# A transformer block and its expert layer on one core: the last loop slots and the router's weights in another order

## The chip, the cores and the metric

The kernel runs on 1 core of one Trainium2 chip. The metric is device time in microseconds (us); lower is better. It is told as the median of several executions, and one more execution was taken with the hardware profiler. Below, PE is TensorE, ACT is ScalarE, DVE is VectorE, POOL is GpSimd, and SP is the engine that issues most transfers.

## The reference

The input is x of 8 x 256 rows of 128 numbers. Cut to what matters:

```
h = layernorm(x) * (1 + ca) + sa
8 layers: Q, K = elu(h Wq)+1, elu(h Wk)+1;  V = Q * sum(K*v) / (Q * sum(K) + eps)
          h = layernorm(gelu(V Wo) + h) * s1 + b1
          h = layernorm(gelu(gelu(h Wf1) Wf2) + h) * s2 + b2
x = x + ga * h
h = layernorm(x) * (1 + cb) + sb
scores = softmax(h Wr) over 8 experts; the two largest of each row are its weights, the others 0
out = x + gb * (shared(h) + sum over experts e of weight[e] * (silu(h Ge) * (h Ue)) De)
```

The shared part is a gated network of the same form with 256 inner columns. It is cut in two, so that there are 10 units of one shape: units 0 and 1 are shared, units 2 to 9 are the experts. All arithmetic is in float32; some products are formed from a rounded high part and a low part of each operand.

## The kernel before

The 2048 rows are cut into 4 chunks of 512, with one chunk in work at a time on each stage. The kernel is written by hand: each engine has a program of its own, in the order in which it runs, and semaphores are the only tie between them. Nothing is reordered by a scheduler, so what stands first in an engine's program and waits also holds all that stands behind it.

**The loop.** One `slot(s, c, l, extra)` of each engine works at four stages of four chunks: `a` is s, the attention products; `b` is s-1, the attention's end; `f` is s-2, the feed-forward net; `d` is s-3, the last norm. There are 32 passes (NI), of 8 layers by 4 chunks. Slots NI and NI+1 stand behind the loop, where stages run out: slot NI has `b`, `f` and `d`, and slot NI+1 only `f` and `d`. `extra` puts work of the next part at named places of a slot.

**Names in a slot.** `ff1(j)` is one quarter of the feed-forward net's first product, in the order 2, 0, 1, 3; `ff2(j)` adds up its second product. PE transposes (`transposes`, L302, four 128 x 128 blocks) bring a norm's rows to one row per partition and back: `y` goes there, `xhB` and `xhD` are the normalised rows of the first and the last norm on their way back. A norm's statistics are `stats_of_rows` (four BN_STATS) and `variance` (five small operations on DVE), then the reciprocal root `rs` on POOL (`rstd`), then `normalize` on DVE. `keep_awake(n, ...)` is n transposes of the identity, whose result nobody reads.

**The second part.** Behind the first attention part chunk c is scaled (`scaled`, `zf`, on ACT), transposed (`zf_to_tm`), and added to the input (`residual`, on DVE). Its norm F gives `xhF`. For chunk 0, `xhF` comes from DVE; for chunks 1 to 3 from ACT (`norm_rows`, which also wants `nbias` from POOL). `norm_to_fm` transposes it, `second_norm` puts it into `hf` on ACT, and `split_h_hi` (ACT) and `split_h` (POOL) make its high and low parts. `scores` is the router's product. The softmax and the choice of two are done on DVE by `route_scores`, `route_compare`, `route_ranks` and `route_weights`, with `exponentials` on ACT. For chunk 0 these use Exp; for the others a quotient of two Silus, so that ACT keeps its table.

**The units.** The last loop goes over i = 0 to 39, with chunk c = i // 10 and unit u = i % 10. For each, PE makes `gate(i)` and `up(i)`, and `down(i - 2)`; ACT takes the Silu of the gate (`sg`); DVE multiplies (`su`), and, for an expert, once more by the weight (`sc`), which PE has spread over all partitions with `broadcast(i)` (L604). `weights_to_fm(c)` transposes the weights, and ACT's `weights(c)` copies them for `broadcast`. `down` from i = 2 on uses high and low parts: ACT copies `sc` to `sc_hi`, POOL subtracts. In the units of chunk c the router's work of chunk c+1 is done. The last chunk's last norm D is also left for the unit loop: `last_to_tm` at i = 12, `normalize("D", ...)` at 13 and `last_to_fm` at 14.

Of the kernel before, what the change touches and what calls it, by code (L numbers as in the profile page):

```python
# [13 lines left out]
P = 128  # L14
NB, L, D = 8, 256, 128
LAYERS, F = 8, 512
E = 8
# [14 lines left out]
def adaln_block(nc, x, w_qkv, w_o, w_f1, w_f2, v_a, v_bo, v_ln1, v_bf1, v_bf2, v_ln2, c_t, w_mod,  # L32
                w_router, w_unit, ident_in, select_in, lower_in, out):

    with ExitStack() as ctx:
# [261 lines left out]
        def _(pe):  # L297
# [38 lines left out]
            def slot(s, c, l, extra=None):  # L336
# [103 lines left out]
                if has(f):  # L440
                    ff1(2)
                    ff1(0)
                if has(b):
# [23 lines left out]
                if has(f):  # L467
                    ff2(1)
                    ff2(2)
                    ff2(3)  # L470
                if has(d) and not has(b):
                    last_norm_to_fm()
                run(extra, "behind ff2")
# [151 lines left out]
            keep_awake(10, ps_v)  # L625
            norm_to_fm(0)
            pe.wait_ge(x_new, 1)
            keep_awake(9, ps_q)
            slot(NI + 1, 1, LAYERS, {"start": scores_0, "behind ff2": unit_0})


            for i in range(CH * U):
# [6 lines left out]
                if i:  # L639
                    gate(i)  # L640
                    up(i)
                    if u == 1:
                        weights_to_fm(c)
                    if i == U + 4:
                        last_to_fm()
# [30 lines left out]
        def _(act):  # L676
# [111 lines left out]
            def norm_rows(c):  # L788
                q = buf("F", c)
                act.wait_ge(nbias_ready, c)  # L790
                act.wait_ge(to_fm["F"], c)
# [23 lines left out]
            def exponentials(c):  # L815
                act.wait_ge(lg_ready, 2 * c + 1)
                if c == 0:
                    nc.scalar.activation(ex[:], lg[:], ACT.Exp).then_inc(ex_ready, 1)
                else:

                    nc.scalar.activation(ex[:], lg[:], ACT.Silu, bias=ones[:, 1:2])
                    nc.scalar.activation(exn[:], lg[:], ACT.Silu, bias=ones[:, 0:1], scale=-1.0).then_inc(ex_ready, 1)
# [18 lines left out]
            def first_scores():  # L841
                second_norm(0)
                split_h_hi(0)
                exponentials(0)
# [5 lines left out]
            slot(NI + 1, 1, LAYERS, {"start": first_scores, "before the last norm": lambda: split_weights_hi(ORDER[7:])})  # L850
            act.wait_ge(ff2_mm, NI)
            nc.scalar.activation(g2[:], ps_f0[:], ACT.Gelu_apprx_tanh, bias=vbf2[:, 0:1]).then_inc(g2_ready, 1)
            for i in range(CH * U):
# [16 lines left out]
                if i == U + 4:  # L870
# [8 lines left out]
                if u == 1:  # L879
                    weights(c)  # L880
                if u == 1 and c:
                    mixture_sum(c - 1)
                if i == 1:
                    scaled(1)
# [14 lines left out]
        def _(pool):  # L899
# [55 lines left out]
            slots(pool, slot, None, {"start": lambda: rstd("I", CH - 1)}, {"start": lambda: split_x_lo(CH - 1, 0)})  # L955
# [7 lines left out]

            def split_h(c):
# [10 lines left out]
            slot(NI, 0, LAYERS, {"end": lambda: rstd("F", 0)})  # L975
# [27 lines left out]
        def _(dve):  # L1003
# [7 lines left out]
            def variance(k, n, eps):  # L1011
# [15 lines left out]
                if k == "F" and n:  # L1027
# [167 lines left out]
            STEPS = 7  # L1195

            def first_step(c):
                return STEPS * c + 2 * max(c - 1, 0)
# [13 lines left out]
            def second_norm(c):  # L1212
                normalize("F", c, x0[:, c])
# [11 lines left out]
            def route_scores(c):  # L1225
                n = first_step(c)
# [7 lines left out]
            def route_compare(c):  # L1234
                n = first_step(c)
# [6 lines left out]
            def route_ranks(c):  # L1242
                n = first_step(c)
# [3 lines left out]
                if c:  # L1247
                    step(n + 4, nc.vector.reciprocal(exn[:], exn[:]))
                    step(n + 5, nc.vector.tensor_tensor(ex[:], ex[:], exn[:], ALU.mult))
                step(n + 4 + 2 * bool(c), nc.vector.tensor_reduce(sm[:], ex[:], AX_X, ALU.add))  # L1250
                nc.vector.reciprocal(rsm[:], sm[:])
                step(n + 5 + 2 * bool(c), nc.vector.scalar_tensor_tensor(out=comb[:], in0=rank[:], scalar=1.5, in1=ex[:],
                                                           op0=ALU.is_lt, op1=ALU.mult))

            def route_weights(c):
                n = first_step(c)
                step(n + 6 + 2 * bool(c), nc.vector.tensor_tensor(comb2[:], comb[:], rsm[:].unsqueeze(2).to_broadcast([P, T, E]),
# [4 lines left out]
                step(n + 7 + 2 * bool(c), nc.vector.tensor_copy(cs[:, :, 0, :].bitcast(F32R), comb2[:]))  # L1262
# [129 lines left out]
```

## Time and profile before

| | |
|---|---|
| median of 3 executions | 525.33 us (525.21 to 526.71) |
| profiled execution | 526.34 us, of which the span is 524.1 us |
| PE busy | 504.4 us, 96% of the span |
| DVE busy | 429.8 us, 82% |
| ACT busy | 405.2 us, 77% |
| POOL busy | 294.6 us, 56% |

The span goes from the first to the last instruction in the trace; 2.24 us lie around it. The loop's slots take about 12 us each. Slot NI begins on PE near 388 us, slot NI+1 near 401 us, the units near 410 us. A matmul's duration in the rows includes the time until its result has landed, and several are under way at once, so the pace is read from start to start.

### The profile page before, as it was taken

The numbers are of one execution on the slowest core, as the hardware profiler recorded it, in microseconds if no ns is written. First come the engines' busy times: TensorE is split into PE (matmuls) and PEld (weight loads), VectorE is DVE, ScalarE is ACT, GpSimd is POOL, SyncE is SP. The second block draws the span as 40 slices with busy tenths as digits, with TensorE's granted clock in tenths as the row PEclk, the third lists the DMA queues.
The fourth block names the chain that finished last, engine by engine and source line by source line (L and its number), as shares of the span: only waits on it lengthen the run. The fifth ranks groups of instructions, "written<-read, shape, count | busy, mean of one in ns | idle before, by whom it ended". The sixth has DMA issues, their size and how long they took to land.

```text
span 524.1 us, 8271 instructions
## 1 busy us (share of the span) xinstructions
PE 504.4 (96%) x1996; PEld 309.3 (59%) x1996; DVE 429.8 (82%) x1633; ACT 405.2 (77%) x603; POOL 294.6 (56%) x327
## 2 busy tenths in 40 slices
PE   7789999999999999999999999999989899899997
PEld 5345565555555555655555555556546477677785
DVE  5889888988898888889888988888887667777754
ACT  4758888888888888888888888888889666657452
POOL 4435655566565666555665656655556376555552
PEclk9989999999999999999999999999999999999999
DMA  8200010001000000100010000001000000000000
GB/s 249 88 16 1 7 41 15 0 5 40 15 5 20 20 15 5 40 15 0 5 40 15 5 20 20 15 5 40 1 0 1 2 0 1 21 1 21 2 21 20
DMA packets 16070, 11.22 MB, mean 21 GB/s; under 512 B 8220, under 2 KB 13852, under 8 KB 16052
## 3 DMA queue, kind: packets, MB, share of 16 engines
q1 hardware_dynamic: 15188, 10.29, 7.1%
q10 hardware_dynamic: 864, 0.73, 0.4%
q8 instruction: 7, 0.11, 0.1%
q14 instruction: 11, 0.09, 0.1%
HBM read 9.96 MB, written 1.05 MB: 21 GB/s over the span
## 4 chain that ended last, share of the span: by engine, by line
PE 82%; DVE 8%; issue 3%; POOL 3%; ACT 2%; DMA 1%; DVEq 0%; POOLq 0%; ACTq 0%
PE bank L436 20%; PE bank L427 15%; PE bank L302 12%; PE bank L448 6%; PE bank L424 5%; PE bank L344 4%; PE bank L349 4%; PE bank L345 4%; PE bank L544 2%; PE bank L546 2%; PE bank L545 2%; PE bank L604 1%; DVE sc L1327 1%; PE bank L589 1%; PE bank L590 1%
## 5 line engine op out<-in xcount | busy, mean ns | idle before, releaser
L436 PE MATMUL bank<-hid,wf 128*128 128x512 f32 x256 | 120.2, 592 | 0.0
L913 POOL TENSOR_TENSOR rsD<-veD,c_half 128x4 f32<-128x4 f32 x32 | 37.3, 1166 | 102.1 <-DVE veD L1025 102.1
L427 PE MATMUL bank<-x,wf 128*128 128x512 f32 x192 | 93.6, 597 | 0.0
L751 ACT ACTIVATE hid<-bank,vbf 128x512 f32<-128x512 f32 x128 | 77.6, 694 | 0.2 <-PE bank L427 0.2
L436 PEld LDWEIGHTS bank<-hid,wf 128*128 128x128 f32 x256 | 46.1, 190 | 46.5 <-issue 31.1
L996 POOL TENSOR_TENSOR xs_lo<-sc,xs_hi 128x512 fp32r<-128x512 f32 x36 | 46.7, 1296 | 45.3 <-ACT xs_hi L869 44.0
L427 PEld LDWEIGHTS bank<-x,wf 128*128 128x128 f32 x192 | 35.3, 191 | 33.4 <-issue 16.3
L1115 DVE TENSOR_SCALAR x<-bank,vln 128x256 f32<-128x256 f32 x64 | 31.9, 540 | 23.8 <-PE bank L302 23.8
L1044 DVE TENSOR_SCALAR xhB<-bank,meanB,rsB 128x128 f32<-128x128 f32 x128 | 43.7, 404 | 8.8 <-POOL rsB L913 8.8
L721 ACT ACTIVATE g<-bank,vbf 128x512 f32<-128x512 f32 x31 | 21.4, 691 | 35.6 <-PE bank L436 35.6
L1044 DVE TENSOR_SCALAR xhD<-bank,meanD,rsD 128x128 f32<-128x128 f32 x128 | 43.7, 404 | 5.0 <-POOL rsD L913 0.7
L302 PEld LDWEIGHTS bank<-ident,y 128*128 128x128 f32 x256 | 29.5, 140 | 26.9 <-POOL y L933 12.9
L344 PE MATMUL bank<-xs_hi,wqkv_hi 128*128 128x512 f32 x87 | 43.7, 502 | 0.9
L933 POOL TENSOR_TENSOR y<-g,xs 128x512 f32<-128x512 f32 x32 | 40.9, 1277 | 6.4 <-ACT g L745 6.3
L913 POOL TENSOR_TENSOR rsB<-veB,c_half 128x4 f32<-128x4 f32 x32 | 32.9, 1028 | 19.7 <-DVE veB L1025 19.7
L745 ACT ACT_TABLE_LOAD x32 | 41.1, 1283 | 0.6
L928 POOL TENSOR_TENSOR y<-g,x 128x512 f32<-128x512 f32 x31 | 39.8, 1283 | 1.8 <-ACT g L721 1.8
L302 PE MATMUL bank<-ident,y 128*128 128x128 f32 x256 | 39.8, 278 | 0.8 <-POOL y L933 0.8
L724 ACT ACT_TABLE_LOAD x31 | 39.8, 1283 | 0.5
L921 POOL TENSOR_TENSOR xs_lo<-xs,xs_hi 128x512 fp32r<-128x512 f32 x29 | 38.3, 1322 | 2.5 <-ACT xs_hi L703 2.5
L448 PE MATMUL bank<-vt,wo 128*128 128x512 f32 x64 | 34.9, 627 | 0.6 <-DVE vt L1131 0.6
L424 PE MATMUL bank<-x,wf 128*128 128x256 f32 x128 | 34.0, 389 | 0.7 <-DVE x L1115 0.7
(178 smaller groups left out, 1181.2 us busy)
## 6 DMA issues: line engine op xcount, KB each, us to landing
wf<-in_w_f SPq DMA_DIRECT2D x16, 256.0 KB, 2.6
wu<-in_w_unit SPq DMA_DIRECT2D x10, 192.0 KB
wqkv<-in_w_qkv SPq DMA_DIRECT2D x7, 192.0 KB, 2.3
x<-in_x SPq DMA_DIRECT2D x4, 256.0 KB, 5.2
out<-ot SPq DMA_DIRECT2D x3, 256.0 KB, 2.2
wo<-in_w_o SPq DMA_DIRECT2D x8, 64.0 KB, 1.8
wmod<-in_w_mod ACTq DMA_DIRECT2D x1, 256.0 KB, 5.4
vln<-in_v_ln SPq DMA_DIRECT2D x16, 1.0 KB, 1.7
```

The source lines that it names most:

```text
L302: mm = nc.tensor.transpose(out_bank[:, j * P:(j + 1) * P], t, ident[:])
L344: nc.tensor.matmul(bank[:], wqkv_hi[:, w], xs_hi[c][:], start=True, stop=False)
L424: mm = nc.tensor.matmul(half(ps_ff[2], h), wf1[:, 2 * P:3 * P], half(x2[(c - 2) % CH], h), start=True, stop=True)
L427: mm = nc.tensor.matmul(ps_ff[j][:], wf1[:, j * P:(j + 1) * P], x2[(c - 2) % CH][:], start=True, stop=True)
L436: mm = nc.tensor.matmul(ps_f0[:], wf2[:, j, :], hid[:, j, :], start=(j == 0), stop=(j == FJ - 1))
L448: nc.tensor.matmul(ps_b[:], wo[:], vt[(c - 1) % CH][:], start=True, stop=True).then_inc(wo_mm, 1)
L745: nc.scalar.activation(g1[:], ps_b[:], ACT.Gelu_apprx_tanh, bias=vbo[:, 0:1]).then_inc(g1_ready, 1)
L751: nc.scalar.activation(hid[:, j, :], ps_ff[j][:], ACT.Gelu_apprx_tanh, bias=vbf1[:, j:j + 1]).then_inc(h_ready, 1)
L913: nc.gpsimd.tensor_tensor(rs[buf(k, n)][:], ve[buf(k, n)][:], c_half[:], ALU.pow).then_inc(rstd_ready[k], 1)
L933: nc.gpsimd.tensor_tensor(y1[:], g1[:], xs[(c - 1) % CH][:], ALU.add).then_inc(y1_ready, 1)
L996: nc.gpsimd.tensor_tensor(sc_lo[k % 2][:], sc[i % 3][:], sc_hi[k % 2][:].bitcast(F32), ALU.subtract).then_inc(sc_lo_ready, 1)
L1044: ap = nc.vector.tensor_scalar(rows_of(k, n)[:, j, :], src[:, j, :], mean[q][:, j:j + 1], rs[q][:, j:j + 1], ALU.subtract, ALU.mult)
```

## The change

**First norm ahead.** In slot NI, DVE's `residual(0)` now stands ahead of the last norm's `normalize`, and the variance of chunk 0's norm F behind that of norm B. POOL does `rs` of B, then `rs` of F and `nbias`. On PE, ten and nine identity transposes become twelve ahead of `xhB` and four behind it; `norm_to_fm(0)` moves from ahead of slot NI+1 into its `ff1`, and the router's product from the slot's start to behind `ff2`.

**Rows by ACT, Silus.** Chunk 0's `xhF` now comes from ACT at the start of slot NI+1; `second_norm(0)` and `split_h_hi(0)` stand behind the first of its four gelus. The Exp, with its table, goes; two Silus stand behind the last gelu. `scaled(1)` moves ahead of that gelu. `weights_to_fm(0)` moves from unit 1 to unit 2.

**Three groups.** `route_ranks` loses its second half to the new `route_sums`, which stands behind the products of the eighth unit, and `route_weights` moves behind those of the ninth. DVE's last `normalize("D", ...)` moves from i = 13 to 14, and PE's `last_to_fm` and ACT's eviction from 14 to 15.

```diff
--- before.py
+++ after.py
@@ -442,0 +443 @@
+                run(extra, "within ff1")
@@ -470,0 +472 @@
+                run(extra, "behind ff2")
@@ -473 +475 @@
-                run(extra, "behind ff2")
+                run(extra, "behind the last norm")
@@ -625,5 +627,7 @@
-            keep_awake(10, ps_v)
-            norm_to_fm(0)
-            pe.wait_ge(x_new, 1)
-            keep_awake(9, ps_q)
-            slot(NI + 1, 1, LAYERS, {"start": scores_0, "behind ff2": unit_0})
+            keep_awake(12, ps_v)
+
+            def awake_0():
+                keep_awake(4, ps_v)
+
+            slot(NI + 1, 1, LAYERS, {"start": awake_0, "within ff1": lambda: norm_to_fm(0),
+                                     "behind ff2": scores_0, "behind the last norm": unit_0})
@@ -642 +646 @@
-                    if u == 1:
+                    if i == 2 or (c and u == 1):
@@ -644 +648 @@
-                    if i == U + 4:
+                    if i == U + 5:
@@ -790,2 +794,3 @@
-                act.wait_ge(nbias_ready, c)
-                act.wait_ge(to_fm["F"], c)
+                act.wait_ge(nbias_ready, c + 1)
+                if c:
+                    act.wait_ge(to_fm["F"], c)
@@ -817,6 +822,2 @@
-                if c == 0:
-                    nc.scalar.activation(ex[:], lg[:], ACT.Exp).then_inc(ex_ready, 1)
-                else:
-
-                    nc.scalar.activation(ex[:], lg[:], ACT.Silu, bias=ones[:, 1:2])
-                    nc.scalar.activation(exn[:], lg[:], ACT.Silu, bias=ones[:, 0:1], scale=-1.0).then_inc(ex_ready, 1)
+                nc.scalar.activation(ex[:], lg[:], ACT.Silu, bias=ones[:, 1:2])
+                nc.scalar.activation(exn[:], lg[:], ACT.Silu, bias=ones[:, 0:1], scale=-1.0).then_inc(ex_ready, 1)
@@ -841 +842 @@
-            def first_scores():
+            def first_rows():
@@ -844 +845,4 @@
-                exponentials(0)
+
+            def last_splits():
+                split_weights_hi(ORDER[7:])
+                scaled(1)
@@ -850 +854,2 @@
-            slot(NI + 1, 1, LAYERS, {"start": first_scores, "before the last norm": lambda: split_weights_hi(ORDER[7:])})
+            slot(NI + 1, 1, LAYERS, {"start": lambda: norm_rows(0), "after the first gelu": first_rows,
+                                     "before the last norm": last_splits})
@@ -852,0 +858 @@
+            exponentials(0)
@@ -870 +876 @@
-                if i == U + 4:
+                if i == U + 5:
@@ -879 +885 @@
-                if u == 1:
+                if i == 2 or (c and u == 1):
@@ -883,2 +888,0 @@
-                if i == 1:
-                    scaled(1)
@@ -955 +958,0 @@
-            slots(pool, slot, None, {"start": lambda: rstd("I", CH - 1)}, {"start": lambda: split_x_lo(CH - 1, 0)})
@@ -963,0 +967 @@
+            slots(pool, slot, None, {"start": lambda: rstd("I", CH - 1)}, {"start": lambda: split_x_lo(CH - 1, 0)})
@@ -975 +979,3 @@
-            slot(NI, 0, LAYERS, {"end": lambda: rstd("F", 0)})
+            slot(NI, 0, LAYERS)
+            rstd("F", 0)
+            norm_bias(0)
@@ -1027 +1033 @@
-                if k == "F" and n:
+                if k == "F":
@@ -1195,4 +1201 @@
-            STEPS = 7
-
-            def first_step(c):
-                return STEPS * c + 2 * max(c - 1, 0)
+            STEPS = 9
@@ -1212,2 +1214,0 @@
-            def second_norm(c):
-                normalize("F", c, x0[:, c])
@@ -1226 +1227 @@
-                n = first_step(c)
+                n = STEPS * c
@@ -1235 +1236 @@
-                n = first_step(c)
+                n = STEPS * c
@@ -1243 +1244 @@
-                n = first_step(c)
+                n = STEPS * c
@@ -1247,4 +1248,6 @@
-                if c:
-                    step(n + 4, nc.vector.reciprocal(exn[:], exn[:]))
-                    step(n + 5, nc.vector.tensor_tensor(ex[:], ex[:], exn[:], ALU.mult))
-                step(n + 4 + 2 * bool(c), nc.vector.tensor_reduce(sm[:], ex[:], AX_X, ALU.add))
+                step(n + 4, nc.vector.reciprocal(exn[:], exn[:]))
+                step(n + 5, nc.vector.tensor_tensor(ex[:], ex[:], exn[:], ALU.mult))
+
+            def route_sums(c):
+                n = STEPS * c
+                step(n + 6, nc.vector.tensor_reduce(sm[:], ex[:], AX_X, ALU.add))
@@ -1252 +1255 @@
-                step(n + 5 + 2 * bool(c), nc.vector.scalar_tensor_tensor(out=comb[:], in0=rank[:], scalar=1.5, in1=ex[:],
+                step(n + 7, nc.vector.scalar_tensor_tensor(out=comb[:], in0=rank[:], scalar=1.5, in1=ex[:],
@@ -1256,2 +1259,2 @@
-                n = first_step(c)
-                step(n + 6 + 2 * bool(c), nc.vector.tensor_tensor(comb2[:], comb[:], rsm[:].unsqueeze(2).to_broadcast([P, T, E]),
+                n = STEPS * c
+                step(n + 8, nc.vector.tensor_tensor(comb2[:], comb[:], rsm[:].unsqueeze(2).to_broadcast([P, T, E]),
@@ -1262 +1265 @@
-                step(n + 7 + 2 * bool(c), nc.vector.tensor_copy(cs[:, :, 0, :].bitcast(F32R), comb2[:]))
+                step(n + 9, nc.vector.tensor_copy(cs[:, :, 0, :].bitcast(F32R), comb2[:]))
@@ -1278,0 +1282 @@
+                select_rounded()
@@ -1280 +1283,0 @@
-                residual_stats(0)
@@ -1282,3 +1285,11 @@
-            slot(NI, 0, LAYERS, {"within the last norm": select_rounded, "after the last norm": residual_0, "within the first norm": lambda: second_norm(0)})
-            slot(NI + 1, 1, LAYERS, {"before the last norm": lambda: route_scores(0),
-                                     "within the last norm": lambda: route_compare(0)})
+            def rows_0():
+                dve.wait_ge(x_new, 1)
+                stats_of_rows("F", 0, x0[:, 0])
+
+            def scores_0():
+                route_scores(0)
+                route_compare(0)
+
+            slot(NI, 0, LAYERS, {"within the last norm": residual_0, "after the last norm": rows_0,
+                                 "within the first norm": lambda: variance("F", 0, EPS_MOD)})
+            slot(NI + 1, 1, LAYERS, {"after the last norm": scores_0})
@@ -1285,0 +1297 @@
+            route_sums(0)
@@ -1300,2 +1311,0 @@
-                    if u == 9:
-                        route_weights(n)
@@ -1305 +1315 @@
-                if i == U + 3:
+                if i == U + 4:
@@ -1331,0 +1342,4 @@
+                if u == 8 and n < CH:
+                    route_sums(n)
+                if u == 9 and n < CH:
+                    route_weights(n)
```

PE at the end of slot NI and the start of slot NI+1, before. `xhF` and `xhB` are the norms' rows; L309 is `keep_awake`, L512 the router's product, L424 and L427 are `ff1`:

```order
L309 MATMUL bank<-ident 128x128 [waits kv_ready]
L309 MATMUL bank<-ident 128x128 x9
L302 MATMUL bank<-ident,xhF 128x128 [waits kv_ready,normedF]
L302 MATMUL bank<-ident,xhF 128x128 x3
L309 MATMUL bank<-ident 128x128 [waits x_new]
L309 MATMUL bank<-ident 128x128 x8
L302 MATMUL bank<-ident,xhB 128x128 [waits normedB]
L302 MATMUL bank<-ident,xhB 128x128 x3
L512 MATMUL bank<-wr,hf 128x8 [waits x_new,hf_ready,ld_moe]
L512 MATMUL bank<-wr,hf 128x8 x3
L424 MATMUL bank<-x_3,wf 128x256 [waits x2_ready] x2
L427 MATMUL bank<-x_3,wf 128x512 [waits g2_ready]
```

The same place of the changed kernel:

```order
L309 MATMUL bank<-ident 128x128 [waits kv_ready]
L309 MATMUL bank<-ident 128x128 x11
L302 MATMUL bank<-ident,xhB 128x128 [waits normedB]
L302 MATMUL bank<-ident,xhB 128x128 x3
L309 MATMUL bank<-ident 128x128 x4
L424 MATMUL bank<-x_3,wf 128x256 [waits x2_ready] x2
L427 MATMUL bank<-x_3,wf 128x512 [waits g2_ready]
L302 MATMUL bank<-ident,xhF 128x128 [waits kv_ready,normedF]
L302 MATMUL bank<-ident,xhF 128x128 x3
L302 MATMUL bank<-ident,y 128x128 [waits x_ready,y2_ready]
L302 MATMUL bank<-ident,y 128x128 x3
L427 MATMUL bank<-x_3,wf 128x512
```

The transposes of `xhF` and the router's product no longer stand ahead of `ff1`, and `xhB` is behind one run of identity transposes only.

ACT from the last gelu of slot NI on (`g`), before; `hid` is the gelus of `ff1`:

```order
L721 ACTIVATE g<-bank,vbf 128x512 [waits ff2_mm]
L784 ACTIVATE hf<-bank,mod,m 128x256 [waits to_fmF]
L784 ACTIVATE hf<-bank,mod,m 128x256
L835 ACTIVATE xs_hi<-hf 128x512 [waits hf_ready]
L818 ACT_TABLE_LOAD
L818 ACTIVATE ex<-lg 128x32 [waits lg_ready]
L751 ACT_TABLE_LOAD
L751 ACTIVATE hid<-bank,vbf 128x512 [waits ff1_mm] x4
L839 ACTIVATE wu_hi<-wu 128x384 x3
L852 ACTIVATE g<-bank,vbf 128x512 [waits ff2_mm]
L859 ACT_TABLE_LOAD
L859 ACTIVATE ek<-bank 128x512 [waits gate_mm]
```

And of the changed kernel:

```order
L725 ACTIVATE g<-bank,vbf 128x512 [waits ff2_mm]
L798 ACTIVATE xhF<-x,nbias,rsF 128x128 [waits nbias_ready]
L798 ACTIVATE xhF<-x,nbias,rsF 128x128 x3
L755 ACTIVATE hid<-bank,vbf 128x512 [waits ff1_mm]
L788 ACTIVATE hf<-bank,mod,m 128x256 [waits to_fmF]
L788 ACTIVATE hf<-bank,mod,m 128x256
L836 ACTIVATE xs_hi<-hf 128x512 [waits hf_ready]
L755 ACTIVATE hid<-bank,vbf 128x512 [waits ff1_mm] x3
L840 ACTIVATE wu_hi<-wu 128x384 x3
L808 ACTIVATE zf<-xs,gt 128x256 [waits to_tmF,x_ready]
L808 ACTIVATE zf<-xs,gt 128x256
L857 ACTIVATE g<-bank,vbf 128x512 [waits ff2_mm]
```

Two table loads and the Exp are gone from between `xs_hi` and `hid`. Four rows of `xhF` are new, and `hf` and `xs_hi` stand behind the first `hid`.

DVE in the units of chunk 0, around the products of the ninth unit (u = 8, `mk`) and the tenth (u = 9, `mq`), before:

```order
L1249 TENSOR_TENSOR ex<-ex,exn 128x32 [waits rt]
L1250 TENSOR_REDUCE sm<-ex 128x4 [waits rt]
L1251 RECIPROCAL rsm<-sm 128x4 [waits rt]
L1252 SCALAR_TENSOR_TENSOR comb<-rank,ex 128x32
L1319 TENSOR_TENSOR mk<-bank,ek 128x512 [waits down_mm,up_mm,sc_lo_ready,sg_ready,rt]
L1327 TENSOR_TENSOR sc<-bank,mk 128x512 [waits bc_mm,su_ready]
L1257 TENSOR_TENSOR comb<-comb,rsm 128x32
L1262 CAST cs<-comb 128x4x8 [waits cst_mm,rt]
L1263 TENSOR_TENSOR cs<-comb,cs 128x4x8 [waits rt]
L1319 TENSOR_TENSOR mq<-bank,eq 128x512 [waits down_mm,sc_lo_ready,up_mm,sg_ready]
L1327 TENSOR_TENSOR sc<-bank,mq 128x512 [waits bc_mm,su_ready]
```

And after:

```order
L1249 TENSOR_TENSOR ex<-ex,exn 128x32 [waits rt]
L1329 TENSOR_TENSOR mk<-bank,ek 128x512 [waits down_mm,up_mm,sc_lo_ready,sg_ready,rt]
L1337 TENSOR_TENSOR sc<-bank,mk 128x512 [waits bc_mm,su_ready]
L1253 TENSOR_REDUCE sm<-ex 128x4
L1254 RECIPROCAL rsm<-sm 128x4 [waits rt]
L1255 SCALAR_TENSOR_TENSOR comb<-rank,ex 128x32
L1329 TENSOR_TENSOR mq<-bank,eq 128x512 [waits down_mm,up_mm,sc_lo_ready,sg_ready,rt]
L1337 TENSOR_TENSOR sc<-bank,mq 128x512 [waits bc_mm,su_ready]
L1260 TENSOR_TENSOR comb<-comb,rsm 128x32
L1265 CAST cs<-comb 128x4x8 [waits cst_mm,rt]
L1266 TENSOR_TENSOR cs<-comb,cs 128x4x8 [waits rt]
```

Three operations (`sm`, its reciprocal, `comb`) have moved behind the first pair of products, and three more (`comb` by the reciprocal, `cs`) behind the second.

## Rows read from the trace of the kernel before

**Rows 1.** The page, part 1: busy us (share of the span) xinstructions
```profile
PE 504.4 (96%) x1996; PEld 309.3 (59%) x1996; DVE 429.8 (82%) x1633; ACT 405.2 (77%) x603; POOL 294.6 (56%) x327
```

**Rows 2.** Timeline, TensorE, last two slots and first unit: start us, us, what
```profile
394.97 0.60 PE L302 MATMUL bank<-ident,y 128*128 128x128 f32 x4
...
398.42 1.25 PE L309 MATMUL bank<-ident 128*128 128x128 f32 x10
...
400.95 0.66 PE L302 MATMUL bank<-ident,xhB 128*128 128x128 f32 x4
...
402.25 1.14 PE L424 MATMUL bank<-x,wf 128*128 128x256 f32 x4
...
406.25 3.60 PE L436 MATMUL bank<-hid,wf 128*128 128x512 f32 x8
409.68 0.60 PE L302 MATMUL bank<-ident,xhD 128*128 128x128 f32 x4
410.12 3.60 PE L542 MATMUL bank<-hf,wu 128*128 128x512 f32 x8
413.55 0.60 PE L523 MATMUL bank<-ident,cs 128*16 128x128 f32 x4
415.63 0.66 PE L302 MATMUL bank<-ident,zf 128*128 128x128 f32 x4 [1.48 <-ACT zf L803]
...
418.61 0.40 PE L544 MATMUL bank<-xs_hi,wu_hi 128*128 128x512 f32 x1
```

**Rows 3.** Timeline, VectorE, same stretch
```profile
397.59 0.17 DVE L1017 TENSOR_TENSOR difB<-stB 128x4 f32<-128x4 f32 x1
...
398.06 0.16 DVE L1025 SCALAR_TENSOR_TENSOR veB<-sqB,dif2B 128x4 f32<-128x4 f32 x1
...
399.53 1.37 DVE L1044 TENSOR_SCALAR xhB<-bank,meanB,rsB 128x128 f32<-128x128 f32 x4 [0.20 <-POOL rsB L913]
```

**Rows 4.** Timeline, GpSimd, same stretch
```profile
396.76 1.02 POOL L913 TENSOR_TENSOR rsF<-veF,c_half 128x4 f32<-128x4 f32 x1 [2.12 <-DVE veF L1025]
...
402.55 1.26 POOL L968 TENSOR_TENSOR xs_lo<-hf,xs_hi 128x512 fp32r<-128x512 f32 x1
...
406.37 1.02 POOL L913 TENSOR_TENSOR rsD<-veD,c_half 128x4 f32<-128x4 f32 x1 [1.60 <-DVE veD L1025]
407.36 2.92 POOL L952 TENSOR_TENSOR wu_lo<-wu,wu_hi 128x384 fp32r<-128x384 f32 x3
```

**Rows 5.** Timeline, ScalarE, same stretch and one chunk later
```profile
400.15 1.02 ACT L784 ACTIVATE hf<-bank,mod,m 128x256 f32<-128x256 f32 x2 [0.42 <-PE bank L302]
401.20 0.63 ACT L835 ACTIVATE xs_hi<-hf 128x512 fp32r<-128x512 f32 x1
...
424.33 1.65 ACT L793 ACTIVATE xhF<-x,nbias,rsF 128x128 f32<-128x128 f32 x4 [0.25 <-POOL nbias L962]
```

**Rows 6.** Timeline, VectorE, end of the first chunk
```profile
435.29 0.19 DVE L1250 TENSOR_REDUCE sm<-ex 128x4 f32<-128x32 f32 x1
...
437.22 0.69 DVE L1327 TENSOR_TENSOR sc<-bank,mk 128x512 f32<-128x512 f32 x1
```

**Rows 7.** Timeline, TensorE, end of the first chunk
```profile
437.19 0.40 PE L592 MATMUL bank<-xs_lo,wu_hi 128*128 128x512 f32 x1
437.96 0.50 PE L604 MATMUL bank<-cst,sel 128*128 128x512 f32 x1 [0.37 <-DVE sc L1327]
438.30 0.39 PE L544 MATMUL bank<-xs_hi,wu_hi 128*128 128x512 f32 x1
```

**Rows 8.** Timeline, TensorE, second chunk, transposes of the two norms
```profile
451.17 0.66 PE L302 MATMUL bank<-ident,xhD 128*128 128x128 f32 x4 [1.11 <-DVE xhD L1044]
...
455.36 0.66 PE L302 MATMUL bank<-ident,xhF 128*128 128x128 f32 x4 [0.54 <-ACT xhF L793]
```

**Rows 9.** Timeline, ScalarE, the eviction between those transposes
```profile
453.01 0.77 ACT L872 ACTIVATE xs<-bank,vln 128x512 f32<-128x512 f32 x1
```

**Rows 10.** Windows of TensorE: stretch, us, busy, granted clock, DMA
```profile
22.00:29.00 7.00, 4.62 (x19) 0.98 0.00 0
29.00:32.00 3.00, 3.00 (x6) 0.50 0.00 0
```

## Prediction

> **What bounds the kernel now.** I read the page first: PE is busy for 96% of the span [rows 1], so only two kinds of change can shorten it: PE work that is no longer issued, and places where PE stands still. The loop itself is not touched, so I followed PE's timeline from slot NI on and looked for rows with an idle time in brackets and for gaps from start to start. They are: the identity transposes between 398.42 and 400.95, which stand in for waiting [rows 2]; 1.48 us before the `zf` transposes at 415.63 [rows 2]; a step of 0.77 us instead of 0.23 before `broadcast` near 438 [rows 7]; and 1.11 us and 0.54 us before the transposes of `xhD` and `xhF` in the second chunk [rows 8]. For each I then looked up what PE waited for on the other engines.
>
> **Part 1, up to the first product of ff1.** From 398.42 to 400.95 PE runs 19 identity and 4 real transposes, 0.110 us each [rows 2]. The end of this stretch is set by `xhB`: DVE starts it at 399.53 [rows 3] and PE its transposes at 400.95, 1.42 later. DVE now has the residual and F's variance out of B's way. B's statistics can start once the `y` transposes (394.97, [rows 2]) have landed at about 395.6. BN_STATS take 0.9, and B's `ve` then stands 0.47 behind its `dif` (397.59 to 398.06, [rows 3]): I get 397.02 instead of 398.06, so 1.04 earlier. Twelve identity transposes end at 398.42 + 1.32 = 399.74, the transposes of `xhB` start at 399.88 (was 400.95). From there to the first `ff1` row it was 1.30 us (400.95 to 402.25), filled with the router's product; it is the way through DVE's eviction, so it stays 1.30 with the fill gone: `ff1` starts at 401.18, 1.07 earlier. Four identity transposes fill 0.44 of that.
>
> **Part 2, ff1 to the first unit.** `ff1` to `ff2` took 406.25 - 402.25 = 4.00; the transposes of `xhF` (0.44) are new in it: `ff2` at 405.62. `ff2` takes 409.68 - 406.25 = 3.43, the router's product now 0.81 more: PE could transpose `xhD` at 409.86 (was 409.68).
> Does what PE wants come in time? ACT's `xhF` wants `nbias`: POOL's `rs` of F follows that of B and ends near 399.35 (1.02 long, [rows 4]), `nbias` near 399.65. Four rows take 1.65 [rows 5]: 401.4, against 403.02, when PE wants them. 1.6 us to spare. The first gelu keeps ACT until 403.8; `hf` and `xs_hi` (1.05 + 0.63, [rows 5]) end at 405.5 instead of 401.83. The second gelu is then done at 406.1, and PE wants it at 405.62 + 0.86 = 406.48: 0.4 to spare.
> POOL is the one that is late. `split_h(0)` waits for `xs_hi`, and behind it in POOL's order stand a weight split and `rs` of norm D. The two take 1.26 and a third of 2.92 [rows 4], 2.22 with their overlap. So `rsD` starts at 405.54 + 2.22 = 407.76, was 406.37. From there 1.02 + 0.11 to DVE and 1.42 to PE: 410.31, so PE waits 0.45. The first unit starts 0.49 later, the step of a stretch that began after a wait: 410.80, against 410.12 [rows 2], **0.68 later than before**.
>
> **Part 3, units 0 to 2.** Before, the first unit's start to that of unit 3 was 418.61 - 410.12 = 8.49 us. In it PE waited from 413.55 + 0.44 = 413.99 to 415.63 for `zf`, since ACT did `scaled(1)` behind the first two Silus and the weights' copy [rows 2]. `zf` is now ready before 410. After: four products 3.44, `zf` 0.44, six products of unit 2 at 0.233, 1.40; the weights' transposes 0.35, `down(0)` 0.86, a wait of 0.07 for ACT's copy and 0.23 for `broadcast`: 6.80, so unit 3 starts at 417.60, **1.01 earlier** than 418.61. What must hold: DVE's chain from the router's product to the first `sc` is longer by two operations and starts late. It starts behind `xhD` at 410.2; by the durations of the same timeline scores and compare take 1.36, ranks 0.44, the reciprocal 0.38, and the product, sums and weights 2.0, so that the first `sc` runs from about 414.2 to 414.9. `up(2)` wants it at 415.38. The Silus that replace Exp (0.3 each) lie behind the gelu's table load that was there before, ahead of a first gate that ends at 411.8; they are free, and would cost 0.5 at most. The removed table loads stood before a gelu for which PE was not waiting, so I count nothing for them.
> Bounds: if POOL were never late (`xhD` in time) the part would give 1.5; if `sc` were 1 us late, or the second gelu, 0.
>
> **Part 4, the handover of chunks.** Three times (chunks 0 to 2; one stands in [rows 7]) PE waits in unit 9 for `sc` of unit 8, because DVE runs sums and `comb` (435.29 to 436.49) ahead of `su` and `sc` [rows 6]. With them behind, `su` starts at 435.29, and `sc`, which starts 0.73 later, ends at 436.7 instead of 437.91; PE wants it at 437.19 + 0.23 = 437.42. The steps become 0.23 + 0.23 instead of 0.77 + 0.34 [rows 7]: 0.65 each, **1.95 in all**. Next in line is `su` of unit 9: sums end at 437.4 to 437.9, so it starts about 0.5 earlier than before. The weights end near 439.9, as the product after them did. Lower bound: 0.37, the idle time alone, each: 1.1. Upper: 1.95.
>
> **Part 5, the last norm D.** Before, PE stood 1.11 before `xhD` and 0.54 before `xhF` [rows 8]. Now both stand next to each other and use one bank, so `xhF` must wait until ACT has evicted `xhD` (0.77, [rows 9]). The 1.11 goes, but `sc` of unit 3 is still behind the statistics on DVE, which I put at 0.56 on `broadcast`; then `xhD` at 453.37, ACT is ready for its eviction at 454.4, `xhF` at 455.2 instead of 455.36 [rows 8]. So the wait mostly changes its place: **0.15 gained**, between 0.5 gained and 1.0 lost.
>
> **Sum.** -1.01 - 1.95 - 0.15 = -3.1. The profiled execution's 526.34 becomes 523.2; it lies 1.0 above the median of the runs, which becomes 525.33 - 3.1 = 522.2. Ends: -1.5 - 1.95 - 0.5 = -3.95 gives 521.4, and 0 - 1.1 + 1.0 = -0.1 gives 525.2.
>
> **A rule against the row.** In part 1, F's five small operations on DVE run while POOL computes `rs` of B. Before, DVE's `dif` of B at 397.59 lay inside POOL's `rs` of F (396.76 to 397.78) and took 0.17 us [rows 3, 4], so I let them run side by side. The Trainium skill, page "SBUF — State Buffer", says under "SBUF: two separate sides" that a VectorE operation with two SBUF inputs and a GpSimd operation exclude each other for a whole instruction. By it F's variance would end about 0.55 later and `xhB` with it, and the sum would be -2.6. By the row it is -3.1, which I take.
>
> **The rivals.**
> - The lock holds for the small operations too. For it: five two-input operations instead of one. Against it: the 0.17 us row. PE is then 0.5 later throughout: 522.7. Chance 0.07. (The rule of the Trainium skill quoted above, page "SBUF — State Buffer", would have it so.)
> - The handover gives little: with the first wait gone, PE meets `sc` of unit 9 or its low part half a microsecond on. DVE's total work there is unchanged. Against it: DVE idles in the next unit, where I find the slack. -1.2 in all: 524.1. Chance 0.12.
> - The front gives nothing: `rsD` or the first `sc` comes a microsecond later than I have it, behind POOL or ACT: -2.1, 523.2. Chance 0.12.
> - PE's clock falls. Identity transposes fall from 19 to 16, with gaps near 400.8 and 410. After a stretch in which PE was busy 4.62 of 7 us the granted clock was 0.50, the 1.2 GHz level, for 3 us [rows 10]; work at it takes twice as long. Such a fall costs 1.5: 523.7 (chance 0.05). Against it: 1.48 us of idle at 415 cost nothing before. It ends slower only if the lower level holds for over 9.4 us, so for all of 401 to 410, since half of it must eat 3.1 and 1.6 more: 527. Chance 0.04.
>
> **How the numbers follow.** The forecast, 522.2 with its own range 521.2 to 523.3, has 0.60. 0.3% is 1.6 us, about what a measurement of this kernel can tell from no change. Faster by more: 0.60 + 0.07 + 0.12 = 0.79; within: 0.12 + 0.05 = 0.17; slower: 0.04. The range of 8 in 10 is 520.9 to 525.0, nearly the ends of the sum.
>
> **What would show it.** Transposes of `xhB` near 399.9 and first `ff1` near 401.2; a wait of about 0.45 for `xhD` near 410; the first unit near 410.8; no wait before `zf`; unit 3 near 417.6; no idle at `broadcast` of unit 9 in chunks 0 to 2; and in chunk 1 one long wait of 1.4 before `xhF`, none before `xhD`. It is wrong if POOL's `rsD` starts after 408.5, if `sc` of unit 0 lands after 415.4, or if the granted clock shows a second low stretch.

## The result, and the profile after

The changed kernel takes 523.33 us, median of five executions (522.12 to 523.49), against 525.33: ratio 0.9948, 95% interval 0.9935 to 0.9960, so it is faster. The medians are 2.0 us apart, which is a ratio of 0.9962 and not 0.9948; the part on the time itself, below, says why a median is a poor measure here. The profiled execution took 523.33 us, its span 521.3; before they were 526.34 and 524.1. The loop ahead of slot NI was not the same length in the two profiles, so I compare from one row on: the transposes of `xhB` in slot NI, at 388.30 before and 388.52 after. From there to the end of the span it was 135.80 and is 132.78: **3.02 us less**. This stretch is called the tail below, and times of after carry 0.22 more than those of before for the same work. The span is given to 0.1 us only. Where hundredths matter I count the gain from the same start to the kernel's last transposes (`yf`, at 520.59 before and 517.79 after), which makes 3.02 as well; a gain below is counted so, and can differ by 0.05 from the difference of two tails. Hundredths can be trusted this far: the transposes of `xhD` in slot NI+1 are 21.38 behind the start of the tail in before, and 21.36 and 21.37 in the two kernels below that leave this stretch as it was.

The page of after, part 1:

```profile
PE 505.4 (97%) x1993; PEld 310.4 (60%) x1993; DVE 425.6 (82%) x1631; ACT 404.2 (78%) x606; POOL 294.5 (56%) x328
```

Timeline of after, TensorE, the stretch of [rows 2]:

```profile
398.64 1.47 PE L309 MATMUL bank<-ident 128*128 128x128 f32 x12
400.03 0.66 PE L302 MATMUL bank<-ident,xhB 128*128 128x128 f32 x4
...
401.32 1.15 PE L424 MATMUL bank<-x,wf 128*128 128x256 f32 x4 [0.20 <-DVE x L1121]
...
403.17 0.60 PE L302 MATMUL bank<-ident,xhF 128*128 128x128 f32 x4
...
410.49 0.66 PE L302 MATMUL bank<-ident,xhD 128*128 128x128 f32 x4 [0.33 <-DVE xhD L1050]
410.98 3.60 PE L544 MATMUL bank<-hf,wu 128*128 128x512 f32 x8
414.42 0.60 PE L302 MATMUL bank<-ident,zf 128*128 128x128 f32 x4
...
417.86 0.39 PE L546 MATMUL bank<-xs_hi,wu_hi 128*128 128x512 f32 x1
```

`xhB` comes 11.51 behind the start of the tail instead of 12.65, the first `ff1` 12.80 instead of 13.95. Then the transposes of `xhF` and the router's product, which before stood ahead of `ff1`, take their time, and PE meets a wait for `xhD` that before did not have. So the first unit is 22.46 - 21.82 = 0.64 later than before. `zf` has no bracket any more, and unit 3 (the last row) starts 29.34 behind the start of the tail instead of 30.31: 0.97 gained.

Where the wait for `xhD` comes from, timeline of after, GpSimd:

```profile
405.71 1.31 POOL L972 TENSOR_TENSOR xs_lo<-hf,xs_hi 128x512 fp32r<-128x512 f32 x1 [2.75 <-ACT xs_hi L836]
406.98 1.00 POOL L956 TENSOR_TENSOR wu_lo<-wu,wu_hi 128x384 fp32r<-128x384 f32 x1
407.94 1.02 POOL L917 TENSOR_TENSOR rsD<-veD,c_half 128x4 f32<-128x4 f32 x1
```

`rsD` could have run from 405.80 on, when DVE's `veD` was done (405.64, 0.16 long), but POOL stood waiting for `xs_hi` with the split in front of it. DVE's `xhD` shows 3.18 of idle time until `rsD` was there.

The handover in after, VectorE, to be read against [rows 6]:

```profile
434.57 0.69 DVE L1329 TENSOR_TENSOR mk<-bank,ek 128x512 f32<-128x512 f32 x1
435.30 0.69 DVE L1337 TENSOR_TENSOR sc<-bank,mk 128x512 f32<-128x512 f32 x1
435.90 0.18 DVE L1253 TENSOR_REDUCE sm<-ex 128x4 f32<-128x32 f32 x1
```

And what PE does with it, against [rows 7]:

```profile
436.24 0.39 PE L592 MATMUL bank<-xs_hi,wu_lo 128*128 128x512 f32 x1
436.47 0.39 PE L594 MATMUL bank<-xs_lo,wu_hi 128*128 128x512 f32 x1
436.70 0.39 PE L606 MATMUL bank<-cst,sel 128*128 128x512 f32 x1
436.93 0.39 PE L546 MATMUL bank<-xs_hi,wu_hi 128*128 128x512 f32 x1
```

`sc` ends at 435.99, and `broadcast` (L606) follows at PE's pace of 0.23, with no bracket.

The last norm D, timeline of after, TensorE, against [rows 8]:

```profile
449.88 0.50 PE L606 MATMUL bank<-cst,sel 128*128 128x512 f32 x1 [0.49 <-DVE sc L1337]
...
452.05 0.60 PE L302 MATMUL bank<-ident,xhD 128*128 128x128 f32 x4
453.90 0.63 PE L302 MATMUL bank<-ident,xhF 128*128 128x128 f32 x4 [1.25 <-ACT xs L878]
```

The brackets of 1.11 and 0.54 have become 0.49 and 1.25: waits that sum to 1.65 before and 1.74 now. What the move is worth is therefore not to be read from brackets; the kernel with this part alone shows it.

### The profile page after: what moved, and what is told of

Its sections match the earlier page's. It is cut to its first block, busy times and chain, and to the rows that moved or that the text cites. A ratio compares the mean times of both kernels' runs of the same rounds, so it can differ in the third digit from the quotient of the medians.

```text
span 521.3 us, 8267 instructions
## 1 busy us (share of the span) xinstructions
PE 505.4 (97%) x1993; PEld 310.4 (60%) x1993; DVE 425.6 (82%) x1631; ACT 404.2 (78%) x606; POOL 294.5 (56%) x328
## 4 chain that ended last, share of the span: by engine, by line
PE 84%; DVE 6%; POOL 4%; issue 3%; ACT 2%; DMA 1%; DVEq 0%; POOLq 0%; ACTq 0%
PE bank L436 19%; PE bank L427 15%; PE bank L302 12%; PE bank L449 6%; PE bank L424 5%; PE bank L344 4%; PE bank L349 4%; PE bank L345 4%; PE bank L546 3%; PE bank L548 3%; PE bank L547 3%; PE bank L591 1%; PE bank L594 1%; PE bank L592 1%; PE bank L606 1%
## 5 line engine op out<-in xcount | busy, mean ns | idle before, releaser
L427 PE MATMUL bank<-x,wf 128*128 128x512 f32 x192 | 93.9, 598 | 0.0
L427 PEld LDWEIGHTS bank<-x,wf 128*128 128x128 f32 x192 | 35.4, 191 | 33.7 <-issue 16.5
L349 PE MATMUL bank<-xs_lo,wqkv_hi 128*128 128x512 f32 x87 | 34.6, 451 | 0.0
```

The source lines that it names most:

```text
L349: return nc.tensor.matmul(bank[:], wqkv_hi[:, w], xs_lo[c][:], start=False, stop=True)
L427: mm = nc.tensor.matmul(ps_ff[j][:], wf1[:, j * P:(j + 1) * P], x2[(c - 2) % CH][:], start=True, stop=True)
```

## The experiments

### The parts one by one

Three kernels have one part of the change each. The first and the third are before with that part added, the second is the changed kernel with the other two parts put back.

**Three groups alone.** `route_sums` and `route_weights` behind the products of units 8 and 9, all else as before. Units are counted from 0 here, as in the code (`u == 8`, `u == 9`); what the texts above call the eighth unit's products are those of u = 8, and the ninth's those of u = 9:

```diff
-                    if u == 9:
-                        route_weights(n)
...
+                if u == 8 and n < CH:
+                    route_sums(n)
+                if u == 9 and n < CH:
+                    route_weights(n)
```

> The kernel before with the third part of the change alone, less the move of norm D: sums behind the eighth unit's products, weights behind the ninth's. The tail is counted from PE's transposes of xhB in slot NI to the span's end; it is 135.8 us in the trace of before and 132.8 in that of the changed kernel. Theory (each of the three chunk handovers lost 0.65 us on PE behind sums and comb, and nothing takes it up): the tail is 1.95 shorter, 133.9, no idle at broadcast near 438, 467 and 494, ratio 0.996. Rival (the wait is taken over by the next product of DVE, half a microsecond on, or the front had to be earlier first): under 0.6 shorter in all, ratio 0.999 to 1.

Measured: 523.29 us, ratio 0.9964 (0.9952 to 0.9977); tail 133.86, a gain of 1.93. TensorE at the end of chunk 0, timeline of this kernel:

```profile
437.35 0.39 PE L592 MATMUL bank<-xs_lo,wu_hi 128*128 128x512 f32 x1
437.58 0.39 PE L604 MATMUL bank<-cst,sel 128*128 128x512 f32 x1
437.81 0.39 PE L544 MATMUL bank<-xs_hi,wu_hi 128*128 128x512 f32 x1
```

Steps of 0.23 throughout, and all three brackets of 0.37 (437.96, 467.31 and 494.08 before) are gone. The saving is 0.65 each and not 0.37: the pace behind a wait is slower for a step, and that goes too. No wait came in their place.

**The front alone.** First norm ahead, rows by ACT, Silus; ranks, sums and weights where they were, and norm D too:

```diff
                     if u == 8:
                         route_ranks(n)
+                        route_sums(n)
+                    if u == 9:
+                        route_weights(n)
...
```

> The changed kernel with its old handover (sums and weights ahead of the products) and its old place of norm D: only the front is changed. Theory (the three parts are independent and add up): unit 3 starts 1.0 us nearer to the transposes of xhB, and all of it is there at the end: tail 134.8 against 135.8 of before, ratio 0.998. Rival (the front's gain is given back in the units, or it is worth more, since the late POOL only takes what would be lost anyway): tail 135.8 or under 134.3.

Measured: 524.24 us, ratio 0.9980 (0.9970 to 0.9990); tail 134.88, a gain of 0.97. The wait for `xhD` is there (0.34), and so are the three brackets at `broadcast`.

**Norm D alone.** `normalize("D", ...)` at i = 14, `last_to_fm` and the eviction at 15:

```diff
-                if i == U + 3:
+                if i == U + 4:
                     normalize("D", NI - 1, tiles(ps_v))
...
```

> The kernel before with norm D alone moved: normalize from i = 13 to 14, last_to_fm and the eviction from 14 to 15. Theory: the wait of 1.1 before xhD goes, and one of about 1.3 comes before xhF and 0.5 before broadcast; the tail changes by -0.15 (135.6). Rival (the move is worth half a microsecond or more by itself, and the handover less): 135.3 or less; or it costs, 136.3 or more.

Measured: 525.16 us, ratio 0.9992 (0.9981 to 1.0002), which times can't tell from no change; tail 135.71, a gain of 0.14. The waits are those of the whole change, timeline of this kernel:

```profile
450.34 0.50 PE L604 MATMUL bank<-cst,sel 128*128 128x512 f32 x1 [0.49 <-DVE sc L1327]
...
454.36 0.63 PE L302 MATMUL bank<-ident,xhF 128*128 128x128 f32 x4 [1.25 <-ACT xs L872]
```

The three gains sum to 1.93 + 0.97 + 0.14 = 3.04 against 3.02: the parts hardly touch each other.

### What the change leaves on the table

**POOL's order.** From the changed kernel, `split_h(0)` and the weight split move behind `rs` of norm D in slot NI+1:

```diff
-            slot(NI + 1, 1, LAYERS, {"behind the sum": first_low_parts})
+            slot(NI + 1, 1, LAYERS, {"end": first_low_parts})
```

> The changed kernel with one line moved on POOL: in slot NI+1 the split of hf and the weight split stand behind rs of norm D instead of ahead of it. Theory (POOL's order makes xhD late, and PE's first unit with it): rsD starts at 405.8 instead of 407.9, the wait of 0.33 before the transposes of xhD goes, first unit 0.45 earlier, tail 132.3 against 132.8. Rival (DVE's router chain or the first sc is the next to be waited for, so the 0.45 come back before unit 3): tail 132.7 to 132.8.

Measured: 521.87 us, ratio to before 0.9933 (0.9920 to 0.9945); tail 132.36, a gain of 0.40 on after. GpSimd, timeline of this kernel:

```profile
404.69 1.02 POOL L917 TENSOR_TENSOR rsD<-veD,c_half 128x4 f32<-128x4 f32 x1 [2.91 <-DVE veD L1031]
405.69 1.27 POOL L972 TENSOR_TENSOR xs_lo<-hf,xs_hi 128x512 fp32r<-128x512 f32 x1
406.91 3.88 POOL L956 TENSOR_TENSOR wu_lo<-wu,wu_hi 128x384 fp32r<-128x384 f32 x4
```

`rsD` runs while POOL waited anyway, and `xs_lo` starts 18.35 behind the start of the tail where it was 17.19 in after: later, but PE shows no wait for it. PE's transposes of `xhD` have no bracket.

**The eviction.** From the changed kernel, unit 15: `last_to_fm` between `gate` and `up`, and ACT's eviction ahead of the unit's Silu:

```diff
                     gate(i)
+                    if i == U + 5:
+                        last_to_fm()
                     up(i)
...
```

> The changed kernel with the transposes of xhD between gate and up of unit 15 instead of behind up, and their eviction on ACT ahead of unit 15's Silu instead of behind it and the copy of sc. Theory (PE's 1.25 us before xhF are the time from xhD's transposes to the end of an eviction that ACT does third): PE works on up (0.7) meanwhile and ACT starts at once, so the wait falls to 0.2 or 0.3 and the tail to 131.8, from 132.8. Rival (ACT's later Silu makes DVE's products and broadcast late, and they are waited for instead): tail 132.5 or more.

Measured, in one execution only: 521.17 us, tail 131.80, a gain of 1.03 on after. TensorE, timeline of this kernel:

```profile
450.00 0.60 PE L302 MATMUL bank<-ident,xhD 128*128 128x128 f32 x4
450.35 0.48 PE L546 MATMUL bank<-xs_hi,wu_hi 128*128 128x512 f32 x1
...
451.56 0.63 PE L302 MATMUL bank<-ident,xhF 128*128 128x128 f32 x4 [0.27 <-ACT xs L864]
```

Three products (the first is shown) now lie where PE stood waiting for the bank, and the bracket falls from 1.25 to 0.27. So the change's wait at this place was the eviction, and no lateness of `xhF` itself. The next kernel has this edit too and shows the same bracket in its trace (0.26); its time is a median of six.

**Both.**

> The changed kernel with both: POOL's rs of norm D first, as in the run before (tail 132.4), and the eviction ahead. Theory: the gains are independent, tail 132.4 - 1.0 = 131.4, ratio to the kernel before 0.9916. Rival as for the eviction alone: 132.2.

Measured: 520.94 us (520.38 to 521.92), ratio to before 0.9921 (0.9908 to 0.9934); tail 131.45, a gain of 1.39 on after, against 0.40 + 1.03 = 1.43. This version beats both kernels.

### The two disputed costs

**The clock.** From the changed kernel, without its 16 identity transposes:

```diff
-            keep_awake(12, ps_v)
...
-                keep_awake(4, ps_v)
+                pass
```

> The changed kernel without its 16 identity transposes between slots NI and NI+1, so that PE stands idle for 1.3 and 0.65 us there. Theory (they are filling, and the granted clock holds without them, as it did in the idle 1.3 us at 388): same tail, 132.8, and a granted clock of 1.00 from 386 us on. Rival (the clock falls to the 1.2 GHz level after the gap, as the prediction's last rival has it): about 3 us at a granted clock of 0.5 behind 400 us, tail 134.3.

Measured: 523.59 us (522.28 to 524.97), ratio to before 0.9958 (0.9942 to 0.9975); tail of the profiled execution 134.48, a loss of 1.69 against after. TensorE, timeline of this kernel:

```profile
399.91 0.63 PE L302 MATMUL bank<-ident,xhB 128*128 128x128 f32 x4 [1.31 <-DVE xhB L1049]
401.18 2.08 PE L424 MATMUL bank<-x,wf 128*128 128x256 f32 x4 [0.64 <-DVE x L1120]
403.05 1.79 PE L427 MATMUL bank<-x,wf 128*128 128x512 f32 x2
404.68 0.60 PE L302 MATMUL bank<-ident,xhF 128*128 128x128 f32 x4
```

And its windows (stretch, us, busy, granted clock, DMA):

```profile
396.00:400.00 4.00, 2.69 (x8) 1.00 0.00 0
400.00:401.50 1.50, 0.86 (x5) 0.89 0.00 0
401.50:404.50 3.00, 3.00 (x6) 0.50 0.00 0
```

`xhB` and the first `ff1` are as far behind the start of the tail as in after (11.59 and 12.86 against 11.51 and 12.80). The whole loss is the way from there to `xhF`: 3.50 instead of 1.85, at the 1.2 GHz level. My theory that the clock holds is out, and the rival stands, for this execution. What PE did before the fall was to stand idle for 1.31, run four transposes and stand idle for 0.64; the 1.33 of idle time alone at 388.32 in the same trace did not do it. This is one trace, and the median alone (523.59 against 523.33) would not have shown the loss. The four executions took 522.28, 523.22, 523.95 and 524.97. The first two fit the times of after, and the other two lie 1.6 to 1.8 above 522.2 and 523.3, so half of them may well have been spared the fall; these have no trace.

**The tables.** From the changed kernel, Exp for chunk 0 again; the second operation only makes ones, so that the rest of the chain stays the same, and one more table load is needed:

```diff
+                if c == 0:
+                    nc.scalar.activation(ex[:], lg[:], ACT.Exp)
+                    nc.scalar.activation(exn[:], lg[:], ACT.Exp, scale=0.0).then_inc(ex_ready, 1)
+                else:
```

> The changed kernel with Exp for chunk 0 in the same place, ahead of the first Silu (the second operand is Exp of 0 times lg, so that DVE's chain is as it is with Silus): one table load of 1.28 us more between the last gelu and the first Silu. Theory of the prediction (table loads were not what PE waited for): the first Silus come 1.3 later, the second sc about 0.9 later, and unit 2 has slack for most of it: tail 132.8 to 133.1. Rival (the Silus in place of Exp are what makes the new order possible): all of it arrives, tail 134.0 or more.

Measured: 522.38 us, ratio to before 0.9949 (0.9935 to 0.9964); tail 132.75, the same as after within 0.04. ScalarE, timeline of this kernel:

```profile
408.72 1.28 ACT L823 ACT_TABLE_LOAD   x1
410.01 0.23 ACT L823 ACTIVATE ex<-lg 128x32 f32<-128x32 f32 x1
...
410.38 1.28 ACT L869 ACT_TABLE_LOAD   x1
411.67 0.60 ACT L869 ACTIVATE ek<-bank 128x512 f32<-128x512 f32 x1
```

Two loads of 1.28 us, and PE loses nothing by the second: ACT has the time here. At this place the Silus instead of Exp are worth nothing by themselves. The kernel does not test the old place, where two loads stood between `xs_hi` and the first gelu; of those only the trace of before speaks, in which PE shows no wait from the first `ff1` (402.25) to the first unit (410.12).

## Why the prediction was right

The sum of -3.1 came out at -3.02 in the tail, and term by term:

- **Part 1.** The first `ff1` 1.07 earlier: it is 1.15 earlier. B's variance did get out of the residual's way, and the way through the eviction stayed as long (1.29).
- **Part 2.** PE waits 0.45 for `xhD`, the first unit 0.68 later: 0.33 and 0.64. `rsD` starts 19.42 behind the start of the tail; by the prediction it was 407.76 - 388.30 = 19.46. That POOL's order, and not DVE, makes this wait is shown by the reordered kernel.
- **Part 3.** Unit 3 1.01 earlier: 0.97. The first `sc` on DVE runs from 414.21, which is 413.99 in the times of before, and was put at 414.2. The table loads were counted at nothing. The kernel with Exp shows this for a load behind the last gelu; for the two at the old place it rests on the trace of before, where PE did not wait.
- **Part 4.** 1.95: 1.93 measured alone. The upper bound was the right one to take, since the steps and not only the brackets shrink. Its rival, that PE meets the next `sc` half a microsecond on, is out. Why the old order made PE wait at all, the prediction had only in part: see the lock, below.
- **Part 5.** 0.15 gained: 0.14. The wait does change its place, to `broadcast` (0.56 expected, 0.49 measured) and to the eviction: `xhF` is at 66.97 behind the start of the tail in the kernel with this part alone, and it was put at 455.2 - 388.30 = 66.90.

**The clock rival** did not come about in the changed kernel. Windows of after, TensorE, for the stretch in which the kernel without identity transposes has its fall:

```profile
401.50:404.50 3.00, 3.00 (x16) 1.00 0.00 0
```

But the experiment shows that it was closer than the chances of 0.05 and 0.04 make it look: 16 identity transposes fewer and it is there in the one execution that was traced, at 1.65 of cost where I had put 1.5. That the transposes left in would suffice I took from one row of 1.48 us of idle time that had cost nothing. That was too little to go by: the same idle times can end in a fall or not, as the last section shows. So part of this forecast was luck.

**The lock rival.** In after, three of F's operations run on DVE wholly within POOL's `rsB` (397.46 to 398.49). VectorE, timeline of after:

```profile
397.65 0.16 DVE L1027 SCALAR_TENSOR_TENSOR dif2F<-difF 128x4 f32<-128x4 f32 x1
397.84 0.16 DVE L1031 SCALAR_TENSOR_TENSOR veF<-sqF,dif2F 128x4 f32<-128x4 f32 x1
397.92 0.16 DVE L1035 SCALAR_TENSOR_TENSOR meanF<-difF,stF 128x4 f32<-128x4 f32 x1
```

Each takes 0.16, and POOL's operation lasts 1.03: no exclusion, so the row was the better guide. It is another matter beside a large operand, as the same trace has it in the second chunk, on VectorE:

```profile
446.89 1.30 DVE L1027 SCALAR_TENSOR_TENSOR dif2F<-difF 128x4 f32<-128x4 f32 x1
```

This `dif2F` began 0.01 behind POOL's `xs_lo` of 128 x 512 (446.88, 1.29 long) and ended with it. The Trainium skill, page "SBUF — State Buffer", section "SBUF: two separate sides", has GpSimd and a VectorE operation with two SBUF inputs exclude each other for a whole instruction. By that rule the trace agrees for `xs_lo` and does not for `rsB`. Why the two differ (the size, or something in what `rs` does) no run here tells.

The rival did not come about in part 1, but the same effect has a hand in part 4, which the prediction overlooked. In before, `comb` of unit 8 runs beside POOL's `xs_lo` and takes 0.85. In after, `comb` of chunk 0 has no such neighbour and takes 0.16. VectorE and GpSimd of before, then VectorE of after:

```profile
435.61 0.85 DVE L1252 SCALAR_TENSOR_TENSOR comb<-rank,ex 128x32 f32<-128x32 f32 x1
435.09 1.32 POOL L996 TENSOR_TENSOR xs_lo<-sc,xs_hi 128x512 fp32r<-128x512 f32 x1 [0.69 <-ACT xs_hi L869]
```

```profile
413.47 0.16 DVE L1255 SCALAR_TENSOR_TENSOR comb<-rank,ex 128x32 f32<-128x32 f32 x1
```

`comb` reads two operands in SBUF and ends 0.05 behind `xs_lo`, and it takes 0.85 at all three handovers of before. Without these 0.69, `sc` would have ended at 437.91 - 0.69 = 437.22, ahead of the 437.42 at which PE wanted it. So, by this estimate, PE's three waits came from one small operation held up beside POOL, and not from the number of operations in front of `sc` alone. The change cures it by taking `comb` out of the way; no run here moves `comb` alone.

**The time itself.** The profiled execution was put at 523.2 and took 523.33. The median was put at 522.2 and is 523.33: within the range of 8 in 10, and 0.03 above the end of the narrower one that had the chance of 0.60. The rival in which the front gives nothing had 523.2, so the time alone would not tell the two apart; the rows do. The median is off because executions of these kernels mostly fall on two levels about 1.1 us apart. Of the five of after three lie at 523.3 to 523.5 and two at 522.1 to 522.4; of the five of before one at 526.71 and four at 525.2 to 525.3 (three of them were known to the prediction). Before was run 34 times more beside the experiments: 23 executions lie at 524.7 to 525.4 (median 525.16) and 11 at 526.1 to 527.0 (median 526.38). Against these the change is worth 2.9 on the lower level and 3.0 on the upper one, as the tail has it; between the medians, where the two kernels stand on different levels, it is 2.0. The step that was off is the subtraction of 3.1 from a median of three, with a profiled execution 1.0 above it as the only hint at the second level. The prediction also took 1.6 us for about what can be told from no change; the intervals here are about 0.6 us to each side, and the front alone (0.2%) was told from none.

## What to carry to other kernels

Read a stall's worth from the steps of PE from start to start, behind the wait too, and not from the bracket alone: 0.37 in brackets was 0.65 each. When a chain is brought forward, look on each engine for what stands idle in front of an operation that others want: here POOL waited 2.75 us for a split that nobody needed yet, with `rsD` behind it, and one line gave 0.40 back. Look also at what runs on POOL beside a small operation of DVE with two operands in SBUF: one took 0.85 us instead of 0.16, and PE waited for what came behind it. Compare traces from a row close to the change on, since the whole span also holds what chance does far ahead of it, and test filler work for the clock by leaving it out, in more than one trace.

## What was not expected of the hardware

The two levels of the profiled executions are made in the prologue. In before the granted clock falls for 3 us from near 29 us on [rows 10]. The kernel with Exp has no such fall. Its windows, TensorE (stretch, us, busy, granted clock, DMA):

```profile
30.00:40.00 10.00, 9.17 (x31) 1.00 0.07 21
```

And of the kernel with the front alone:

```profile
10.00:20.00 10.00, 8.54 (x22) 0.84 0.62 203
20.00:30.00 10.00, 7.35 (x36) 1.00 0.00 0
```

In each profile PE stands idle for a good part of its first 30 us (busy 21 to 24 of them). Where the granted clock then falls to the 1.2 GHz level near 29 us, as in before and after and two others, the work that follows is late, and slot NI is reached at 388.3 to 388.5. Where it fell only near 10 us, with transfers still coming in (four profiles), or in neither place (two), slot NI is reached at 387.1 to 387.4. This holds for all ten profiled executions, of kernels whose first 380 us are the same.

What PE does just before 29 us does not decide it. Timeline of before, TensorE:

```profile
27.54 0.66 PE L302 MATMUL bank<-ident,xhB 128*128 128x128 f32 x4 [0.92 <-DVE xhB L1044]
28.92 2.05 PE L424 MATMUL bank<-x,wf 128*128 128x256 f32 x4 [0.73 <-DVE x L1115]
```

And of the kernel with the front alone:

```profile
27.44 0.66 PE L302 MATMUL bank<-ident,xhB 128*128 128x128 f32 x4 [0.92 <-DVE xhB L1050]
28.83 1.10 PE L424 MATMUL bank<-x,wf 128*128 128x256 f32 x4 [0.73 <-DVE x L1121]
```

The idle times are the same, and the product behind them takes 2.05 in the one and 1.10 in the other. The next transposes of `xhB` come at 40.56 and 39.46, so 1.0 of the 1.08 between these two profiles at slot NI (388.30 and 387.22) arises here. So the place of one fall of 3 us is worth 1.1 us, more than either of the two smaller parts of this change (0.97 and 0.14), and it differs from execution to execution of one kernel.

That the levels of the run times are these same two is argued and not shown: those executions have no trace. It fits that a mean granted clock of 0.999 or 1.000 stands beside 13 of the 23 lower executions of before, and beside none of the 11 upper ones (0.993 to 0.997).
